# Transposing the stacked queries and keys with DMAs from SBUF in place of TensorE, in a one-layer transformer kernel

## The reference

```python
h = token_table[x] + pos + segm_table[mask]            # 8 x 1024 x 192
qkv = layernorm(h) @ qkv_weight.T                      # 12 heads of 16
q, k = layernorm_over_16(q) * 16 ** -0.5, layernorm_over_16(k)
h = h + (softmax(q @ k.T) @ v) @ proj_weight.T         # full attention within a sequence
y = gelu(quant(layernorm(h)) @ quant(w1).T * alphas + b1)
h = h + quant(clip(y, -10, 10)) @ quant(w2).T * alphas2 + b2
```

## Time and profile before

| | us |
|---|---|
| median of three runs | 1113.6 (1111.63 to 1113.84) |
| profiled execution, own time | 1112.17 |
| its span | 1110.2 |
| PE busy | 972.4 (88%) |
| ACT busy | 868.3 (78%) |
| DVE busy | 814.5 (73%) |
| POOL busy | 432.5 (39%) |
| first exponential starts | 97.90 |

### The profile page before, as it was taken

The page is one execution under the profiler, slowest core; times in us unless marked ns, Lnnn a source line. Parts: engine busy times, 40 slices in busy tenths (PEclk is TensorE's granted clock), DMA queues, the critical chain, the costliest instruction groups (busy, mean ns, idle before and its releaser), DMA issues.

```text
span 1110.2 us, 19437 instructions
## 1 busy us (share of the span) xinstructions
PE 972.4 (88%) x7535; PEld 380.3 (34%) x7535; DVE 814.5 (73%) x2289; ACT 868.3 (78%) x936; POOL 432.5 (39%) x354
## 2 busy tenths in 40 slices
PE   1246999999999999999999999999999999989883
PEld 1132333333434342433434343424334343413131
DVE  6486556978878786969788787869697787815265
ACT  0244788889798979889898979788897989798961
POOL 3766161263534443453635344443535312201011
PEclk9985999999999999999999999999999999999995
DMA  8421010020301112020302031020303000000000
GB/s 206 75 26 22 9 22 9 1 44 1 66 7 30 16 40 33 1 44 1 72 2 35 9 57 16 19 26 1 44 1 44 1 16 1 16 1 15 1 15 14
DMA packets 26681, 29.37 MB, mean 26 GB/s; under 512 B 5056, under 2 KB 23168, under 8 KB 26592
## 3 DMA queue, kind: packets, MB, share of 16 engines
q0 software_dynamic: 18432, 12.59, 9.8%
q1 hardware_dynamic: 7184, 14.86, 4.2%
q10 hardware_dynamic: 976, 0.70, 0.3%
HBM read 21.85 MB, written 6.29 MB: 25 GB/s over the span
## 4 chain that ended last, share of the span: by engine, by line
PE 42%; ACT 33%; DVE 15%; POOL 4%; issue 4%; DMA 2%; POOLq 0%; SPq 0%; DVEq 0%; ACTq 0%
ACT probs L535 25%; PE ps_o L890 15%; PE ps_s L873 9%; PE ps_j L918 4%; ACT gelu L529 4%; PE ps_j L970 3%; POOL stack L462 3%; PE ps_j L931 3%; PE ps_j L926 2%; PE ps_j L937 2%; ACT L529 2%; PE ps_j L956 2%; ACT L535 2%; PE ps_j L941 2%; DVE stack L655 1%
## 5 line engine op out<-in xcount | busy, mean ns | idle before, releaser
L535 ACT ACTIVATE probs<-ps_s 128x1024 f32<-128x1024 f32 x768 | 736.2, 1024 | 125.4 <-PE ps_s L873 118.4
L890 PE MATMUL ps_o<-probs,v_sb 128*32 128x512 f32 x3072 | 396.1, 607 | 0.0
L873 PE MATMUL ps_s<-qT,kT 64*128 64x512 f16 x1536 | 266.8, 386 | 37.7 <-ACT probs L535 27.0
L462 POOL TENSOR_TENSOR stack<-sq,stack 128x384 f16<-128x384 f32 x128 | 123.7, 987 | 148.8 <-DVE stack L655 148.8
L873 PEld LDWEIGHTS ps_s<-qT,kT 64*128 64x128 f16 x1536 | 62.5, 93 | 305.8 <-ACT probs L535 270.9
L471 POOL TENSOR_TENSOR y_sb<-y_sb,b_row 128x768 f32<-128x768 f32 x16 | 29.1, 1817 | 277.5 <-DVE y_sb L729 277.5
L409 POOL DMA_INDIRECT h_all<-in_L_tok_token_table,idx x64 | 103.0, 1610 | 73.9 <-DMA h_all<-in_L_tok_segm_table,idx 59.3
L890 PEld LDWEIGHTS ps_o<-probs,v_sb 128*32 128x32 f32 x3072 | 69.4, 109 | 124.3 <-issue 116.1
L409 POOL DMA_INDIRECT h_all<-in_L_tok_segm_table,idx x64 | 99.8, 1560 | 26.7 <-issue 15.5
L453 POOL TENSOR_TENSOR sq<-qk 128x384 f32<-128x384 f32 x56 | 46.3, 827 | 146.2 <-DVE qk L692 146.2
L529 ACT ACTIVATE gelu<-ps_j,b_sb,s_sb 128x512 f32<-128x512 f32 x96 | 70.1, 775 | 26.3 <-PE ps_j L956 25.3
(11 more groups left out here) (122 smaller groups left out, 1057.4 us busy)
## 6 DMA issues: line engine op xcount, KB each, us to landing
h_all<-in_positions SPq DMA_DIRECT2D x8, 768.0 KB
out<-h_all SPq DMA_DIRECT2D x16, 384.0 KB
qT<-in_L_ffn_w SPq DMA_DIRECT2D x2, 576.0 KB, 8.1
h_all<-in_L_tok_segm_table,idx POOLq DMA_INDIRECT x64
h_all<-in_L_tok_token_table,idx POOLq DMA_INDIRECT x64
probs<-in_L_attn_qkv_weight SPq DMA_DIRECT2D x2, 432.0 KB, 4.9
probs<-in_L_ffn_alpha_a ACTq DMA_DIRECT2D x1, 384.0 KB, 5.0
probs<-in_L_attn_proj_weight SPq DMA_DIRECT2D x1, 144.0 KB, 5.7
```

The costliest lines, as they stand in the source:

```text
L462: last = nc.gpsimd.tensor_tensor(low, src, high, ALU.subtract)
L535: nc.scalar.activation(probs[:, u % PROBS, 2 * pair:2 * pair + 2], ps_s[:, 2 * pair:2 * pair + 2], ACT.Exp, scale=SCORE_SCALE).then_inc(ex ...
L873: last = mm(ps_s[:, j], kT[rows, par, head // 2, m * P:(m + 1) * P], qT[rows, par, head // 2, nh * NQ:(nh + 1) * NQ], start=True, stop=True)
L890: last = mm(ps_o[32 * j:32 * j + 2 * D, :], v_sb[:, par, m, (GH * group + j) * VE:(GH * group + j) * VE + 2 * D], probs[:, u % PROBS, j], ...
```

## The change

Jobs D and E are gone from PLAN and FIRST_PLAN. SP gets a new function, `turn`: for each tile of a half it waits until POOL has written the low parts and issues two DMAs with `transpose=True`, straight from `stack` to qT and to kT, 128 x 768 float16 each. They count on four new semaphores, one per tile. `stack` has four slots instead of two. The scores of the first unit of an even half-step wait for all four; DVE's high parts of tile t wait for the DMAs of that tile of the half before. In the SP list, `turn` of half s + 2 stands behind the store of half-step s. The other jobs stand at other places of PLAN.

```diff
--- before.py
+++ after.py
 PLAN = """
-h h o
-Y0 Y1 Y2 F0 Y3 w0 F1
+h h
+o Y0 Y1 F0 Y2 F1
...
-JOB_KINDS = "ABCDEFGHIWXY"
+JOB_KINDS = "ABCFGHIWXY"
...
-A0' A1' A2' A3' B0' B1' n0 n1 r0' r1' D0 E0 n2 B2' D1 E1 n3 B3' r2' C0' D2 E2 r3' D3 E3 S0'
-n0' n1' C1' C2' C3' D0' E0' n2' D1' E1' n3' D2' E2' D3' E3'
+A0' A1' A2' A3' B0' B1' n0 n1 r0' r1' n2 B2' n3 B3' r2' C0' r3' S0'
+n0' n1' C1' C2' C3' n2' n3'
...
-        stack = sb("stack", [P, 2, 2, H, 4, D], F16)
+        stack = sb("stack", [P, TH, 2, H, 4, D], F16)
...
+        turned = [sem(f"turned{t}") for t in range(TH)]
...
-            if kind == "D":
-                return [(qT[:, par, :, here], six(ps16))]
-            if kind == "E":
-                return [(kT[:, par, :, here], six(ps16))]
...
-                yield stack[:, t % 2, n, :, high, :], stack[:, t % 2, n, :, low, :], src
+                yield stack[:, t, n, :, high, :], stack[:, t, n, :, low, :], src
...
+            def turn(half):
+
+                par = half // 2 % 2
+                if half // 2 >= 2:
+
+                    sp.wait_ge(scores_mm, 2 * UNITS * (half // 2 * 2 - 2))
+                if half == 2:
+
+                    sp.wait_ge(job_mm["W"], HB)
+                for t in range(TH):
+                    at = (half % 2 * TH + t) * P
+                    sp.wait_ge(stack_ready, nth(half, t, TH))
+                    for n, dst in enumerate((qT, kT)):
+                        sp.dma_start(out=dst[:, par, :, at:at + P], in_=stack[:, t, n].rearrange("p h a d -> p (h a d)"),
+                                     transpose=True).then_inc(turned[t], 16)
+
             def one(s0, s, b):
+                store(s0, s, b)
+                if job_runs("T", s0):
+                    turn(job_half("T", s))
+
+            def store(s0, s, b):
                 if not job_runs("Y", s0):
                     return
...
+            for half in range(2):
+                turn(half)
             halfsteps(one)
...
+                    if t < 2 and job_half("B", s0):
+
+                        pool.wait_ge(stack_ready, half * TH + (t - 1))
...
-                if TH * h0 + t >= 2:
-
-                    dve.wait_ge(job_mm["E"], half * TH + (t - 1))
+                if h0:
+
+                    dve.wait_ge(turned[t], 32 * half)
...
                 if u == 0 and nh == 0:
-                    pe.wait_ge(job_out["D"], (s + 2) * TH)
-                    pe.wait_ge(job_out["E"], (s + 2) * TH)
+                    for t in range(TH):
+                        pe.wait_ge(turned[t], 32 * (s + 2))
...
-                if kind in "DE":
-                    pe.wait_ge(stack_ready, nth(half, t, TH))
-                    for i in range(H // 2):
-                        src = stack[:, t % 2, "DE".index(kind), 2 * i:2 * i + 2].rearrange("p h a d -> p (h a d)")
-                        last = nc.tensor.transpose(bank16((kind, t), s0, F16)[:, i * P:(i + 1) * P], src, ident_h[:])
```

More of the change, by code:

```diff
@@ L77 @@
 PLAN = """
-h h o
-Y0 Y1 Y2 F0 Y3 w0 F1
-G0 F2 F3 H0 G1 P0
-h h
-G2 G3 W0 W1 W2 H1 H2 H3
-h l0 h R0
-W3 m0 h
-W4 h
-h N0 W5 I0
-I1 h o A0
-I2 h A1 A2
-h A3 I3
-C0 B0 X0
-X1 B1 r0 X2 X3 B2 X4 X5 r1 B3 h r2 h r3 g h
-h
-h S0 n0
-h n1 o
-D0 x0 E0 C1
-n2 h C2 D1
-E1 n3 h
-D2 h x1
-h D3 E2 x2
-E3 x3 x4 h
-x5 C3 h
+h h
+o Y0 Y1 F0 Y2 F1
+w0 G0 F2 F3 H0 G1
+h P0 h
+G2 W0 H1 G3 H2 W1
+H3 h l0
+Y3 W2 R0 h m0
+W3 h
+h W4 W5
+N0 h I0
+h A0 o A1 A2
+B0 h
+I1 I2 I3 h B1 X0 X1
+A3 X2 X3 B2 X4 X5 g B3 r0 C0 r1 h h h
+h
+h
+r2 r3 S0 h n0 o
+h n1 x0 n2 n3
+h
+C1 C2
+x1 x2 h x3 x4
+h x5
+h
+C3 h
 """
-JOB_KINDS = "ABCDEFGHIWXY"
+JOB_KINDS = "ABCFGHIWXY"
 UNIT_WORK = [[] for _ in range(UNITS)]
@@ L137 @@
 IN_TURN = [w for w in JOBS if w[0] not in "XB"]
-LAG = {**dict.fromkeys("PNABCDE", 2), **dict.fromkeys("FGHIX", -1), "Y": -2, "W": 0}
-PER_HALF = {**dict.fromkeys("ABCDEFGHIY", TH), **dict.fromkeys("XW", HB)}
+LAG = {**dict.fromkeys("PNABCT", 2), **dict.fromkeys("FGHIX", -1), "Y": -2, "W": 0}
+PER_HALF = {**dict.fromkeys("ABCFGHIY", TH), **dict.fromkeys("XW", HB)}
 def job_half(kind, s):
@@ L176, in copied_by_act @@
 def copied_by_act(kind, part, s0):
-    return s0 < 0 and kind in "ABCD"
+    return s0 < 0 and kind in "ABC"
 def layer(nc, x_tok, x_seg, tok_table, seg_table, w_qkv, w_proj, w1, b1, aw1, aa1, w2, b2, aw2, aa2,
@@ L317, in copies @@
         def copies(s0, s, kind, t):
-            if kind not in "ABCDEGI":
+            if kind not in "ABCGI":
                 return []
@@ L326, in copies @@
             two = lambda a: a[0:KC, 0:2 * P].rearrange("p (k n) -> p k n", k=2)
-            six = lambda a: a[:, 0:H // 2 * P].rearrange("p (i n) -> p i n", n=P)
-            here = slice(tile * P, (tile + 1) * P)
             if kind == "A":
@@ L452, in square @@
                         pool.wait_ge(summed, half * TH + (t - 1))
+                    if t < 2 and job_half("B", s0):
+                        pool.wait_ge(stack_ready, half * TH + (t - 1))
                     nc.gpsimd.tensor_tensor(sq[:, t % 2], qk[:, t], qk[:, t], ALU.mult).then_inc(squared, 1)
             def split_low(s0, s):
-                if not job_runs("D", s0):
+                if not job_runs("T", s0):
                     return
                 for t in range(TH):
-                    pool.wait_ge(high_ready, nth(job_half("D", s), t, TH))
+                    pool.wait_ge(high_ready, nth(job_half("T", s), t, TH))
                     for high, low, src in stack_parts(t):
@@ L643, in split_qk @@
             def split_qk(s0, s, t):
-                half, h0 = job_half("D", s), job_half("D", s0)
+                half, h0 = job_half("T", s), job_half("T", s0)
                 g = lambda a: a.rearrange("p (g d) -> p g d", d=D)
@@ L811, in work @@
                     qk_roots(s0, s)
-                elif kind == "n" and job_runs("D", s0):
+                elif kind == "n" and job_runs("T", s0):
                     split_qk(s0, s, t)
```

## The result

The changed kernel took 1143.3 us (median of 4 runs, 1141.4 to 1150.5) against 1113.0 for the kernel before (4 runs of the same session): a ratio of 1.0285, 95% interval 1.0238 to 1.0333. The forecast was 1134 with a range of 1086 to 1235.

A forecast was written before the change was run, and what follows sets the result against it. ACT was taken to set the pace, with POOL's list the new bound. Removed and moved work -21.3 us, late DMAs +37.8 in the loop and +4.0 ahead of it, gave +20.5 and 1134 us, range 1086 to 1235.

The forecast's parts named there:

- ACT sets the pace: Half-step: ACT busy 53.04 of 61.66 us, so the change's worth is read from its 7.8 us of waits for scores.
- What is removed: PE's transposes and DVE's copies go; ACT's waits where they stand, 1.8 us a half-step, can go.
- What is moved, early units: Up to the scores of unit 6, the new list is shorter by 1.43 us a half-step.
- POOL's chain: POOL starts at 16.0 us, gathers end 37.7, squares 41.2; `o` is late, ACT resumes at 48.6, half-step 60.4 us.
- The price is that POOL's addition waits for Y3: Y3 moved behind unit 6's scores, ending at 15.4 us, so POOL's addition begins at 16.0 us of the half-step.
- The DMAs: +37.8 in the loop, +4.0 ahead of it: Transposing DMAs land 5.4 us late in each of seven even half-steps, +37.8 us; first tiles ahead of the loop, +4.0 us.
- S: Time per transposing DMA in SP's queue, taken as 1.70 us, keeping 0.62 and 5.0; forecast case 1.42 to 2.3, chance 0.30.
- 72S - 101.9: Total change in us for other S above 1.05, zero at S = 1.42.
- the first rival: The DMAs keep pace, S at or under 1.03: no even half-step waits, 0 to 1 us won ahead, 1092 us; chance 0.25.
- the third rival: Between: S from 1.03 to 1.42, short waits eat what was won, 1092 to 1113 us; chance 0.16.
- the fourth: `o` isn't late as POOL's gathers go faster, DMAs keep pace: another 1.5 us in eleven half-steps, 1076 us; chance 0.03.
- By the packet: DMAs paid by the packet, S = 2.6: 12.6 us in seven half-steps, 18.4 ahead, 1199 us; at 5.0, 1372; chance 0.26.

The follow-up runs named there:

- the old plan: Changed kernel, transposes still by DMA, with the plan of the kernel before, D and E struck out: 1091.5 us, 0.9805 of the kernel before.
- the run with the norms first: Changed kernel with Y3 back in unit 1, norms of all four tiles ahead of x0, C1 and C2, and `o` behind n2: 1139.0 us.
- the run with the norms spread: Changed kernel with Y3 back in unit 1 and the norms spread, S0 and n0 in unit 15, n1 to n3 in units 16 to 18: 1088.05 us.
- With Y3 back: Changed kernel with one job moved, Y3 back in unit 1 behind F0: 1094.3 us, 0.9839 of the kernel before.
- removing half of them: Changed kernel with the key's transposing DMAs issued for the first two steps only, later scores using stale keys: 1136.4 us.
- the runs without additions: Changed kernel without POOL's first addition (bias b2): 1110.1 us; with both of POOL's 128x768 additions left out, one element added instead: 1085.6 us.
- the halved DMAs: Changed kernel with each transposing DMA of 768 columns issued as two of 384: 1225.8 us, 1.1006 of the kernel before.

## Why the prediction was right or wrong

**ACT sets the pace; read its waits.** Right. ACT's busy time in a half-step is nearly the same, and the difference between the half-steps is in the units listed above.

**What is removed: up to 1.8 us a half-step.** Right, and the one gain that came: units 18 to 23 lose 2.0 us of waits. Under the old plan, where unit 19 keeps 0.49 of them, the change is worth 21 us.

**What is moved, early units: 1.43 us.** Mis-sized. Units 1 to 9 lost 0.4 us of waits. I had counted the shortened lists in full. Only unit 5's wait shrank (1.14 to 0.61 us); unit 2's went from 1.34 to 1.84 in odd half-steps and 0.84 in even ones, which began late, and unit 7 got one of 0.20.

**POOL's chain.** Its times came out: the additions at 16.4 us of the half-step (forecast 16.0), the last gather ended at 37.9 (37.7), the last square at about 42 (41.2). What was to follow, ACT waiting at unit 18 for a late `o`, did not: ACT was already late by units 10 to 12, and ran without a gap from unit 14 on. The link is real, as the run with the norms first shows, but hidden: the term that the forecast put at 48.6 us for unit 18 never bound.

**The step that failed** is the sentence "The price is that POOL's addition waits for Y3". I priced when POOL starts, and not what DVE runs beside it. The first instruction behind Y3's eviction in DVE's list is the root chain, and two of its instructions wait for the two additions: 3.15 us a half-step, 46.4 in all. The -21.3 us for what is removed and moved came out as a cost of 13 to 23: 30.3 less the 7 to 17 us of the DMAs (below). In the trace of before, collisions of this kind were to be seen: the pair of casts of the second tile took 1.95 us beside POOL's low parts, where the first tile's took 0.63:

```profile
506.42 1.95 DVE L655 CAST stack<-sq 128x384 f16<-128x384 f32 x2
```

I didn't ask which instruction they would hit next. Nor does the prediction have a term for TensorE's clock, which fell behind the waits that followed.

**The DMAs: +37.8 in the loop, +4.0 ahead of it.** Mis-sized twice, in opposite directions. S was 1.33, not 1.70, and landing took 1.5 us after the last issue, not 3.11. With tiles ready as forecast nothing would have been late by more than 1 us, and the run with the norms spread shows it: last tile ready at 55.5 us, 0.9 us late. But in the changed kernel it was ready at 58.6 to 59.1 us in most half-steps, not 54.9. The first tile was 0.7 to 1.2 us late, and the fourth came 9.3 us behind it, where the forecast has 6.3: between the norms DVE copies `o`, for which it waits, and quantises x0 beside POOL, with two instructions of 1.02 us each that take 0.49 and 0.43 alone. This is not Y3's doing. With Y3 back the last tile is ready at 56.1 us of a half-step that is 3 us shorter, and most even half-steps wait 2.2 us all the same. In the changed kernel they waited 14.9 us more than odd ones. The first exponential came 2.0 us later (99.89 against the earlier trace rows), but in nine other runs that have the same work ahead of the loop it came at 97.07 to 98.93, so this is no sure cost of the DMAs, and the +4.0 is not borne out. By these waits the DMAs cost 15 to 17 us, and removing half of them returned 7.

**The sum.** By the runs: DMAs in the old plan -21, the rest of the new plan +3, Y3 +49, together +31 against 30.3 measured. These are steps from one run to the next and must add up, so the sum proves nothing by itself; that Y3's +49 is for the most part the held chain is shown by the runs without additions. The forecast of +20.5 came near by luck, since two errors of opposite sign nearly cancelled: 25 to 35 us too much for the DMAs, 34 to 44 too little for the plan. The line 72S - 101.9 also counts a growing gain ahead of the loop for S under 1.45, where the first rival allows 1 us; at S = 1.70 this doesn't matter.

**Rivals.** The forecast's own condition, S from 1.42 to 2.3, did not hold. S = 1.33 is the third rival's, "between", at 1092 to 1113 us; its condition came true and its time didn't, because of Y3. "The DMAs keep pace", 1092 us, is the time of the kernels with Y3 in unit 1, 1091.5 and 1094.3, though S is above the 1.03 that it asked for and the second of them still waits 2.2 us at most even starts. In the fourth, `o` is in time because POOL's gathers go faster. No unit waited for `o` here either, but because ACT was late already; the gathers ended as forecast. "By the packet" was refuted by the halved DMAs: the price is by the DMA. The Trainium skill ("DMA: Bandwidth & Descriptors", "Latency and other measured facts") gives 261 GB/s, from which the prediction estimated 0.75 us. Here 196.6 KB every 1.33 us is 148 GB/s, set by SP's issue, so for DMAs of this size the measurement decides against that figure.

## What to carry to other kernels

When a job moves, list what the other engines run at its new time, and not only when it starts and who waits for it. An instruction of POOL on 768 columns that overlaps a serial chain of tiny DVE instructions of the kinds that are held (next section) costs the chain nearly its whole length, 1.5 to 1.64 us of 1.82 here. Look at the granted clock behind every new wait of PE. And test a bundled change in its parts first: here one word of the plan hid a gain of 18 us.
